# Perceiver layer on one core: the first stage by chunks inside attention's program, queries two pairs ahead

## The reference

```python
x = x + _L0_xattn_ref(_layernorm(x, axis=-1), ctx_768, w_q, w_kv, w_out, b_out)
x = x + _L0_attn_ref(_layernorm(x, axis=-1), ...)      # a decayed running sum over the 64 tokens
x = x + _L0_ffn_ref(_layernorm(x, axis=-1), w1, b1, w2, b2)

def _L0_xattn_ref(query, context, w_q, w_kv, w_out, b_out):
    q = query @ w_q
    k, v = jnp.split(context @ w_kv, 2, axis=-1)       # 16 heads of 64
    attn = jax.nn.softmax(jnp.einsum('bhqd,bhkd->bhqk', q, k) * SCALE, axis=-1)
    out = jnp.einsum('bhqk,bhkd->bhqd', attn, v)
    return out.transpose(0, 2, 1, 3).reshape(B, NQ, INNER) @ w_out + b_out
```

## Time and profile before

| what | us |
|---|---|
| median of 3 runs (lowest to highest) | 2390.58 (2389.76 to 2395.09) |
| the profiled execution's own time | 2392.82 |
| its span in the trace | 2391.0 |
| PE busy | 2296.6 |
| DVE busy | 1831.3 |
| POOL busy | 1614.5 |
| ACT busy | 1546.9 |

### The profile page before, as it was taken

The page is one execution under the profiler, slowest core; times in us unless marked ns, Lnnn a source line. Parts: engine busy times, 40 slices in busy tenths (PEclk is TensorE's granted clock), DMA queues, the critical chain, the costliest instruction groups (busy, mean ns, idle before and its releaser), DMA issues.

```text
span 2391.0 us, 44126 instructions
## 1 busy us (share of the span) xinstructions
PE 2296.6 (96%) x13696; PEld 2099.4 (88%) x13696; DVE 1831.3 (77%) x3670; ACT 1546.9 (65%) x2690; POOL 1614.5 (68%) x834
## 2 busy tenths in 40 slices
PE   4968999999999999999999999999999999889999
PEld 3647999999999999999999999999999998878888
DVE  7767777777777777777777777777777777779884
ACT  4655666666667666667666666666666666555444
POOL 2006887888888888888888888888888886421111
PEclk9989999999999999999999999999999999999999
DMA  5867888888888888888888888888888887877000
GB/s 156 241 195 168 196 198 193 197 198 199 199 203 199 202 199 201 199 198 199 199 199 199 201 200 200 200 200 200 199 202 199 201 194 163 210 187 195 18 10 27
DMA packets 384766, 438.93 MB, mean 184 GB/s; under 512 B 81856, under 2 KB 355648, under 8 KB 384704
## 3 DMA queue, kind: packets, MB, share of 16 engines
q1 hardware_dynamic: 368880, 427.23, 75.4%
q10 hardware_dynamic: 15824, 10.91, 1.9%
HBM read 167.42 MB, written 52.43 MB: 92 GB/s over the span
## 4 chain that ended last, share of the span: by engine, by line
POOL 38%; PE 22%; issue 21%; SPq 4%; DVE 4%; DMA 2%; ACT 1%; POOLq 0%; ACTq 0%; DVEq 0%
POOL p_pt_lo L771 21%; PE p_scores L1461 7%; POOL p_nat L798 6%; POOL p_q_lo L783 5%; PE p_acc L1477 4%; POOL p_ct_lo L779 4%; POOL p_ct_hi L790 3%; SPq L655 3%; PE p_scores L1627 2%; PE p_cols L1614 2%; PE p_acc L1479 2%; PE p_scores L1581 2%; PE p_cols L1523 1%; DMA p_raw<-o_scratch 1%; PE p_scores L1539 1%
## 5 line engine op out<-in xcount | busy, mean ns | idle before, releaser
L771 POOL TENSOR_TENSOR p_pt_lo<-p_landed,p_pt_hi 128x768 fp32r<-128x768 f32 x504 | 991.6, 1990 | 321.6 <-ACT p_pt_hi L912 321.6
L1477 PE MATMUL p_acc<-p_nat,p_pt_hi 128*128 128x384 f32 x3024 | 887.4, 360 | 9.2 <-POOL p_pt_lo L771 7.2
L1479 PE MATMUL p_acc<-p_nat,p_pt_lo 128*128 128x192 f32 x3024 | 758.2, 251 | 0.0
L1461 PE MATMUL p_scores<-p_ct_hi,p_q_hi 128*128 128x512 f32 (+2 forms) x2048 | 705.2, 348 | 26.7 <-DVE p_ct_hi L1400 13.9
L948 ACT ACTIVATE p_prob<-p_scores,p_negmax 128x800 f32<-128x800 f32 (+1 forms) x512 | 471.5, 926 | 398.1 <-DVE p_negmax L1212 397.9
L1461 PE MATMUL p_scores<-p_ct_hi,p_q_lo 128*128 128x512 f32 (+2 forms) x2048 | 704.6, 347 | 0.0
L1477 PEld LDWEIGHTS p_acc<-p_nat,p_pt_hi 128*128 128x128 f32 x3024 | 567.5, 188 | 18.3 <-POOL p_pt_lo L771 9.0
L1479 PEld LDWEIGHTS p_acc<-p_nat,p_pt_lo 128*128 128x128 f32 x3024 | 577.0, 191 | 0.0
L912 ACT ACTIVATE p_pt_hi<-p_landed 128x768 fp32r<-128x768 f32 x504 | 398.9, 839 | 165.9 <-PE p_acc L1481 124.0
L1461 PEld LDWEIGHTS p_scores<-p_ct_hi,p_q_hi 128*128 128x128 f32 x2048 | 390.2, 191 | 72.7 <-issue 14.3
L1220 DVE STREAM_TRANSPOSE turned<-p_prob 128x1536 f32<-128x1536 f32 x256 | 452.7, 1768 | 0.0
(11 more groups left out here) (228 smaller groups left out, 3116.1 us busy)
## 6 DMA issues: line engine op xcount, KB each, us to landing
p_landed<-turned SPq DMA_DIRECT2D x2032, 104.0 KB, 2.3
resid<-in_ctx SPq DMA_DIRECT2D x128, 288.0 KB, 5.0
o_scratch<-resid SPq DMA_DIRECT2D x256, 96.0 KB, 2.7
qk_scratch<-p_out_a SPq DMA_DIRECT2D x16, 1024.0 KB, 4.6
p_stage<-qk_scratch SPq DMA_DIRECT2D x31, 512.0 KB, 3.9
p_stage<-qk_scratch SPq DMA_DIRECT2D x62, 256.0 KB, 4.3
p_stage<-in_ctxT SPq DMA_DIRECT2D x31, 401.0 KB, 4.6
p_stage<-in_ctxT SPq DMA_DIRECT2D x62, 200.5 KB, 5.6
```

The source lines that it names most:

```text
L771: nc.gpsimd.tensor_tensor(pt_lo[:, t0:t1, :, :], by_tile(slot, t0, t1), bits(pt_hi[:, t0:t1, :, :]), ALU.subtract).then_inc(pt_lo_done, 1)
L1461: last = nc.tensor.matmul(scores[:, S0 + lo:S0 + hi], w, x, start=m == 0, stop=m == len(terms) - 1)
L1477: nc.tensor.matmul(acc[k % 2][:, 0:2 * DC], pt_hi[:, t, :, :].rearrange("p i x -> p (i x)"), x[:, t, :], start=t == 0, stop=False, skip_gr ...
L1479: nc.tensor.matmul(acc[k % 2][:, 0:DC], pt_lo[:, t, :, :].rearrange("p i x -> p (i x)"), x[:, t, 0:DC], start=False, stop=False, skip_grou ...
```

## The change: what it does

The two blocks become one (whole_layer). What is computed is the same, and so are the pairs, the chunks, and everything behind the first scores.

- **Start.** x is loaded by chunks of 512 tokens, the query weights in halves, the key weights in quarters, in the order in which they are needed. Statistics, root, inverse and normalising are done by chunks too. DVE normalises chunk 0; POOL normalises chunks 1 to 3, between the lo parts of the weights. The inverse takes four instructions in place of five. All transposes use one PSUM bank.
- **Pairs.** The queries have three banks, and PE makes the queries of pair g + 2 before it multiplies pair g with the keys. The pairs are written out without a loop. The stack buffer is still two deep.
- **Stores.** Every pair is stored by itself, from four buffers of one pair each (before: four of two pairs each), so a contiguous run in DRAM has 512 bytes in place of 1024, and SP issues 64 store DMAs in place of 32.
- **First batch.** Its hi and lo parts are made during the pairs, by ACT and, in place of DVE, POOL. The second batch's context is loaded at pair 8.
- **Between the stages** no engine waits for all others; the first scores' products stand in PE's order right behind the last pair's. SP waits for all stores to land before it goes into the batches.
- **DVE** has 64 empty instructions (engine_nop) at its very start.

```diff
-    write_queries(nc, e["x"], e["w_q"], e["wkT"], e["qk_dram"], e["ctx_in"], e["ctxT_in"], shared, turned)
-    assert nc.sbuf_base <= turned_at
...
+    SLOTS, QPS = 4, 3
+    WKP = 4
+    XLN = 2 * CTT + 5
...
+        xp, qp = scores[:, 0:512], [scores[:, (1 + i) * 512:(2 + i) * 512] for i in range(QPS)]
+        ap, bp = acc, [cols[i][0:DCB, :] for i in range(2)]
...
+            def store_queries(g):
+                c, j = divmod(g, HP)
+                sp.wait_ge(evac_act, 2 * g + 2)
+                sp.wait_ge(evac_dve, 2 * g + 2)
+                for buf, rows in zip(staged[g % SLOTS], (slice(0, P), slice(P, DC))):
+                    dst = qk_dram[c * CB:(c + 1) * CB, rows, j * 2 * NQ:(j + 1) * 2 * NQ].rearrange("b c n -> c b n")
+                    sp.dma_start(dst, buf[:, :, :, :].rearrange("p b h q -> p b (h q)")).then_inc(qk_stored[g % SLOTS], 16)
...
+            load_tokens(0)
+            load_query_weights(0)
+            load_key_weights(0)
+            load_query_weights(1)
+            for i in range(1, WKP):
+                load_key_weights(i)
+            for c in range(1, NC):
+                load_tokens(c)
+            sp.wait_ge(zeroed, 1)
+            sp.dma_start(first_a[:, 0:NKV], ctxT_in[0, 0:P, :]).then_inc(first_a_in, 16)
+            for half in (slice(0, DCB), slice(DCB, P)):
+                sp.dma_start(first_b[half, 0:NKV], ctxT_in[0, P:DC, :]).then_inc(first_b_in, 16)
+            sp.dma_start(first_odd, odd_key(ctx_in, 0)).then_inc(first_odd_in, 16)
+            for g in range(GP):
+                store_queries(g)
+                if g == HP + 1:
+                    for done in qk_stored:
+                        sp.wait_ge(done, 2 * 32)
+                    sp.dma_start(first_q[:, 0, :], qk_dram[0, 0:P, :]).then_inc(first_q_in, 16)
+                    for half in (slice(0, DCB), slice(DCB, P)):
+                        sp.dma_start(first_q[half, 1, :], qk_dram[0, P:DC, :]).then_inc(first_q_in, 16)
+                if g == HP:
+                    sp.wait_ge(padded, 1)
+                    for h in range(2):
+                        load_ct_a(1, h, stage[:, h, :])
+                if g == (NC - 1) * HP - HP // 4:
+                    sp.wait_ge(xp_ready, NC * KB)
+                    for dst, src in raw_pieces(raw, ctx_in, 0):
+                        sp.dma_start(dst, src).then_inc(first_raw_in, 16)
+            for done in qk_stored:
...
+            query_weights_lo(0); key_weights_lo(0); query_weights_lo(1)
+            key_weights_lo(1); x_normalised(1); key_weights_lo(2); key_weights_lo(3)
...
+            x_normalised(2)
+            for h in range(2):
+                first_context_lo(h)
+            x_normalised(3)
+            for k in range(KB):
+                first_queries_lo(k)
+            for h in range(2):
+                first_rows_lo(h)
...
+            x_roots(0); query_weights(0); key_weights(0); x_hi(0); x_hi(1); query_weights(1); x_roots(1)
+            for g in range(GP):
+                c, j = divmod(g, HP)
+                stack_high(g)
+                if g > 0:
+                    evacuate_act(g - 1)
+                if c == 0 and j in (0, 1, 2):
+                    key_weights(j + 1)
+                if c + 2 < NC and j == 6:
+                    x_roots(c + 2)
+                if c + 1 < NC and j in (3, 4):
+                    x_hi(KB * (c + 1) + j - 3)
+                if c == 1 and j in (0, 1):
+                    first_context(0, j)
+                if c == 1 and j in (6, 7):
+                    first_context(1, j - 6)
+                if c == 2 and j in (6, 7):
+                    first_queries(j - 6)
+                if c == NC - 1 and j in (2, 4):
+                    first_rows((j - 2) // 2)
+            evacuate_act(GP - 1)
...
+            def x_inverse(c):
+                step, cols_of = c * XLN + 2 * CTT + 1, slice(c * CTT, (c + 1) * CTT)
+                v, w, u, inv = (x_std[:, n, cols_of] for n in range(4))
+                dve.wait_ge(x_root, c + 1)
+                nc.vector.reciprocal(u, w).then_inc(x_step, 1)
+                dve.wait_ge(x_step, step + 1)
+                nc.vector.tensor_tensor(u, u, v, ALU.mult).then_inc(x_step, 1)
+                dve.wait_ge(x_step, step + 2)
+                nc.vector.scalar_tensor_tensor(u, w, 0.25, u, ALU.mult, ALU.add).then_inc(x_step, 1)
+                dve.wait_ge(x_step, step + 3)
+                nc.vector.reciprocal(inv, u).then_inc(x_step, 1)
...
+            for _ in range(64):
+                dve.engine_nop()
+            x_statistics(0, range(CTT)); x_inverse(0); x_normalised(0); x_lo(0); x_lo(1); x_statistics(1, range(CTT))
+            for g in range(GP):
+                c, j = divmod(g, HP)
+                stack_low(g)
+                if g == 0:
+                    x_inverse(1)
+                else:
+                    evacuate_dve(g - 1)
+                if c + 2 < NC and 2 <= j < 6:
+                    x_statistics(c + 2, (j - 2,))
+                if c + 2 < NC and j == 7:
+                    x_inverse(c + 2)
+                if c + 1 < NC and j in (3, 4):
+                    x_lo(KB * (c + 1) + j - 3)
+            evacuate_dve(GP - 1)
...
+            def queries(g):
+                c, j = divmod(g, HP)
+                if c == 0 and j in (0, HP // 2):
+                    pe.wait_ge(wq_lo_done, 1 if j == 0 else 2)
+                if j == 0:
+                    pe.wait_ge(xp_lo, (c + 1) * KB)
+                if g >= QPS:
+                    pe.wait_ge(stack_lo, 2 * (g - QPS + 1))
+                cols_of = slice(c % 2 * CT, (c % 2 + 1) * CT)
+                terms = [(w, xv, k) for k in range(KB) for w, xv in ((wq_hi, xT_hi), (wq_lo, xT_hi), (wq_hi, xT_lo))]
+                for n, (w, xv, k) in enumerate(terms):
+                    last = nc.tensor.matmul(qp[g % QPS], w[:, k, j * P:(j + 1) * P], xv[:, k, cols_of], start=n == 0, stop=n == len(terms) - 1)
+                last.then_inc(q_ready, 1)
...
+            x_turned(0); x_turned(1); queries(0); queries(1)
+            for g in range(GP):
+                c, j = divmod(g, HP)
+                if c + 1 < NC and j in (3, 4):
+                    x_turned(KB * (c + 1) + j - 3)
+                if g + 2 < GP:
+                    queries(g + 2)
+                with_keys(g)
...
+                elif k == 0:
+                    pe.wait_ge(evac_act, 2 * GP)
+                    pe.wait_ge(evac_dve, 2 * GP)
```

More of the change, by code:

```diff
@@ L710, in body @@
                         load_ct_a(n + 2, 0, stage[:, 0, :])
-            sp.wait_ge(padded, 1)
-            for h in range(2):
-                load_ct_a(1, h, stage[:, h, :])
+            load_tokens(0)
[28 more added lines that the diff above has]
+            for done in qk_stored:
+                sp.wait_ge(done, GP // SLOTS * 32)
             passes(sp, body)
```

460 lines of the change are left out of this document (196 added, 264 removed).

## The result

The changed kernel takes **2356.43 us** (median of four runs, 2352.52 to 2358.57), the kernel before 2392.48 in the same comparison: ratio 0.9848, 95% interval 0.9827 to 0.9868. The time lies in the forecast range, 3.8 us above the forecast value. The profiled execution took 2358.56 us; forecast were 2354.8.

What follows compares the result with a forecast made beforehand. PE's losses ahead of the first row maximum were taken as the bound; start 18.0, pairs 111.9 and change of stage 4.8 put it at 134.7 us in place of 172.72, 38.0 less: 2352.6 us, range 2345 to 2364.

Steps and rivals of the forecast that it cites:

- Start: Before PE's first query-weight product: it would start at 18.0 us in place of 33.20, 15.2 us won, bounds 11 to 19.
- rival 3: At the start: POOL misses normalising, empty instructions are free, 4.6 us less, fewer stalls 3 more: 2345 to 2348 us; chance 0.08.
- Pairs: PE's 32 pairs: 102.7 + 3.0 + 2.2 + 4.0 us of stalls = 111.9 us in place of 117.2, gain 5.3.
- So these waits go: In the pairs: queries two pairs ahead remove the 9.3 us of waits between engines; new stalls taken as 4 us.
- rival 5: In the pairs: queries two ahead do nothing, as DVE is full; stalls stay at 9.3 us, 2358 us; chance 0.06.
- The rule on GpSimd: In the pairs: up to three DVE inverses each wait for one 2 us POOL instruction, adding some 2 to 4 us.
- Change of stage: From the last pair to the first row maximum: 4.8 us in place of 22.3, gain 17.5.
- Rival 2: Behind the first maximum: late-landing stores delay the moves by 3 to 8 us, 2356 to 2361 us; chance 0.12.
- Stores: DMA queue during the pairs: 2.9 us a pair, below 3.21; extra loads fill the queue, but nothing is counted for it.
- at full clock throughout: Sign in the new profile: PE runs without a clock drop, last key product near 130 us, first maximum near 135.
- rival 1: In the pairs: stores bind at 3.3 to 3.4 us a pair, PE waits 5 to 12 us, 2358 to 2365; chance 0.15.
- rival 4: In the batch loop: code no longer stays resident, each round waits; at 4 us a round 2409 us; chance 0.04.

## Why the prediction was right, and where it wasn't

**Start: right.** 18.0 us forecast, 18.18 measured. The terms too: normalising 1.3 + 3.5 us forecast, 4.89 measured, and 1.39 with POOL out of the way, which shows the cause. Two terms had the wrong size with little effect. The data landed at 5.04 us and not at 4.6. And I let the 64 empty instructions end 0.7 us behind the data, at 0.073 us each; they end at 3.0 us, 0.035 us from one to the next, before the data. Two figures don't follow from the terms: the lower bound of what is won (11 us; with 3.9 us of POOL in place of 3.5 it would be 14.8), and the 4.6 us of rival 3, where 3.5 and 0.7 are 4.2.

**Pairs: right in the sum without the rows, for a reason that was half wrong.** "So these waits go" was put down to queries two pairs ahead. Undoing that alone costs 0.5 us ahead of the rows' wait (0.6 at the first maximum). The finer hand-over of the halves takes the same waits away: undoing it alone costs 3.8 us, undoing both 6.7. The forecast didn't cost it, and the list of the change ahead of the prediction doesn't name it. So rival 5's first half (two ahead does nothing) was nearly true in this kernel, and not because DVE was full, but because another part of the change did the work already. Without that part two ahead would have been worth 3.0 us. The sum came out once the rows' wait is gone (111.8 against 111.9 us). By difference, 111.8 less the other three terms as forecast, 3.9 us of stalls are left where I took 4; with bounds of 1 and 9.3 us that this fits so well is in part luck.

**The rule on GpSimd: it holds, at one place.** The Trainium skill ("SBUF — State Buffer", "Who interferes with whom") has DVE instructions with two SBUF inputs locked out while a GpSimd instruction that reads SBUF runs. L1141 lasted 1.74 us beside L589's 1.85 for chunk 1, and 0.16 and 0.18 for the chunks 2 and 3. For chunk 2 POOL rested. For chunk 3 the trace has POOL's L600 beside L1141 until 0.01 us before its end, and nothing was held; with the rough spans of POOL I can't say why. Not three inverses wait, but one, and the sum didn't grow: the run without the rows has the time that I took without the rule.

**Change of stage: right.** 4.8 us forecast, 4.9 measured from the first score, and the moves 12.0 us behind. Rival 2 didn't happen.

**Stores: the step that failed.** "I count nothing for it in the likeliest case" was wrong by 5 us. The price of the stores was good: with stores alone in the queue of the changed kernel, 80 to 96 us, a share of 0.95 for five pairs makes 3.0 us a pair against 2.9 forecast. I even had the queue "full nearly throughout". What I drew from it was wrong: I looked at the four buffers as what a full queue would hit, and they were never waited for. It hit the one transfer with a date, the rows: asked for at 105.3 us, wanted at 111.7, there at 115.45, and ACT, which works in order, carried the delay to all. Six loads issued together needed 10.1 us; in the kernel before, with store runs of 1024 bytes, they needed 11.8 us (99.3 to 111.1) and nobody waited for them. So what failed is the date, 6.4 us behind the request, more than the price of the short runs. PE stood for 3.69 us, and the half clock behind that made it 5: "at full clock throughout" was wrong as well. So a part of rival 1 came true, through another door and with 5 us in place of 5 to 12. Leaving the load out, taking the rows later and storing in long runs each shortened it, by 5.1, 4.2 and 3.0 us.

**The loop: right by luck, for a reason that I didn't have.** Rounds of 117.2 us against 117.0. I named the loss of resident code but argued against it only with the unchanged count of instructions. The run without empty instructions shows that this was no argument: the count is unchanged there too, and it costs 24 us. With the 64 it stays away. So rival 4 was a real danger that I gave 0.04, though smaller than I made it: 1.7 us a round and not 4, which would have left the kernel faster than before. The forecast for this program held because the change already had a count that works.

The forecast time itself came out 3.8 us low because errors offset each other: 5.0 us too little ahead of the first maximum, 1.8 us too little behind it, and 3.1 us given back by the end, which differs from one execution to the next.

**What is open.** Ahead of the first maximum the miss is accounted for, but why the clock falls behind one hole and not behind another is open: it fell behind holes of 2.17, 2.79 and 3.69 us, and stayed behind others of 1.51, 2.17 and 2.71. And of the 5.1 and 4.2 us that two runs won there, the medians show 1.2 and 0.7 (as ratios to the kernel before on the same chip, 0.9852 and 0.9841 beside 0.9848). With runs from 2350 to 2358 us, medians of four or five can't settle whether that is scatter or given back; in the trace of the run with the rows taken late, the pieces behind the first maximum are 1881.5 and 331.5 us, so nothing is given back in it. What exactly in the code's layout makes DVE fetch its loop again is open as well.

## What to carry to other kernels

Where a queue will be full, don't ask only whether buffers run out: list the transfers that someone waits for at a given place in an in-order engine, and put that place later, which cost at most one longer pair here (4.3 us in place of 3.2). A hole in PE can cost more than its length: look at the granted clock behind it. Where three engines hand work around in a ring, first hand over in halves, and test depth and hand-over apart and together: here most of what depth would have won, 3.0 us, the hand-over had won already. And when straight code ahead of a loop grows, look at the instruction queues between two instants inside the loop: packets in every round there are worth a try with empty instructions; here one count of three helped.

## What the hardware showed that I hadn't expected

- **Code that is fetched again in each round**: 57 fetches of 8.2 KB in 1400 us without empty instructions, none with 64, 58 with 128; a round 118.9 in place of 117.2 us.
- **GpSimd holds DVE instructions with one SBUF tensor input too.** L1150 and L1151 (one tensor and two columns of numbers) are the same four instructions: 4.89 us beside POOL, 1.39 us without. L1132, one tensor and a constant, took 1.07 us beside L584 in the start of chunk 1 and 0.17 elsewhere.
- **The end differs from one execution to the next.** The code behind the last row maximum is the same in the changed kernel and in the two with the rows taken late, yet took 335.3, 331.5 and 340.1 us. Windows of the changed kernel, of the one with the rows taken late, and of that with GpSimd's wait as well:
```profile
2070.00:2080.00 10.00, 8.96 (x54) 7.81 (x54) 5.11 (x8) 5.89 (x13) 8.40 (x9) 1.00 1.14 261
2080.00:2090.00 10.00, 7.84 (x36) 6.86 (x37) 8.58 (x23) 6.87 (x13) 0.27 (x1) 0.83 0.75 172
```
```profile
2070.00:2080.00 10.00, 8.10 (x49) 6.93 (x48) 8.31 (x18) 6.95 (x12) 5.28 (x5) 1.00 0.90 219
2080.00:2090.00 10.00, 7.54 (x44) 6.54 (x45) 8.71 (x17) 8.74 (x18) 4.24 (x4) 1.00 0.59 148
```
```profile
2070.00:2080.00 10.00, 5.60 (x37) 4.79 (x35) 4.78 (x7) 5.78 (x11) 5.66 (x5) 1.00 1.03 180
2080.00:2090.00 10.00, 9.27 (x38) 8.05 (x39) 7.51 (x23) 5.76 (x11) 0.59 (x1) 0.66 0.64 158
```
  In the last of them PE is busy for 5.60 us of ten beside a DMA share of 1.03, and in the ten behind it the mean granted clock is 0.66, a part of them at 1.2 GHz in place of 2.4; PE then needs 9.27 us for 38 products. The run that kept full clock there is the shortest. The rest of the end differs too, so this shows one place and not the whole 8.6 us. So in these three executions a few microseconds at the same place of the end came out differently each time; how often it does in runs without a trace, I can't say.
